# Four graph layers on one core: the adjacency products of the last two layers with features stationary and the adjacency moving

## The reference

```
1: relu((I - D A_sym D) (h W))                          A_sym = relu((A + A.T) / 2)
2: softmax over neighbours(leaky(s1 + s2)) (h W)
3: h = relu(A (h Wg0 + bg0)); h = relu(A (h Wg1 + bg1))
   then four LSTMs over windows of 1, 2, 3, 4 nodes write parts of h anew
4: A_hat = dinv (A + I) dinv; z = (A_hat h) W1.T
   out = batchnorm(relu(batchnorm(z)) W2.T)
```

## Time and profile before

| | us |
|---|---|
| median of 3 runs | 3378.92 (3371.41 to 3380.02) |
| the profiled execution | 3374.21 |
| its span in the profile | 3372.0 |

### The profile page before, as it was taken

One profiled execution on the slowest core, in us unless ns is written; L12 is line 12 of the kernel. 1 busy time (PEld: TensorE's weight loads), 2 busy tenths in 40 slices (PEclk: granted clock), 3 DMA queues, 4 the chain that ended last, 5 costly groups with the idle time before them and its releaser, 6 DMA issues. The chain is left out here.

```text
span 3372.0 us, 39977 instructions
## 1 busy us (share of the span) xinstructions
PE 2826.8 (84%) x14962; PEld 2369.5 (70%) x14962; DVE 1708.4 (51%) x2868; ACT 1273.6 (38%) x2136; POOL 222.4 (7%) x121
## 2 busy tenths in 40 slices
PE   1328999859899994999979999698989885999977
PEld 1216888759899993788867878576768674777743
DVE  3874454456767663222232222388787874333336
ACT  3763222245555553111121111266767664111115
POOL 0220111100000100000000000001000000000000
PEclk8558999979999996999989999899999997999979
DMA  7875333231322224111132111301121025223238
GB/s 293 291 264 201 131 122 139 89 132 39 109 67 63 76 56 157 70 57 63 68 144 82 56 63 67 119 13 38 26 75 50 26 63 189 93 94 118 100 129 315
DMA packets 237887, 366.34 MB, mean 109 GB/s; under 512 B 8752, under 2 KB 190272, under 8 KB 216896
## 3 DMA queue, kind: packets, MB, share of 16 engines
q1 hardware_dynamic: 235456, 360.51, 31.2%
q10 hardware_dynamic: 2304, 4.20, 0.3%
HBM read 226.12 MB, written 138.55 MB: 108 GB/s over the span
## 5 line engine op out<-in xcount | busy, mean ns | idle before, releaser
L1040 PE MATMUL n_acc<-n_hb,n_p 128*128 128x129 f32 x4096 | 484.5, 281 | 47.5 <-DVE n_u L998 30.9
L1040 PEld LDWEIGHTS n_acc<-n_hb,n_p 128*128 128x128 f32 x4096 | 478.4, 197 | 49.0 <-issue 28.5
L679 PE MATMUL l_acc<-l_g_hi,l_a_hi 128*128 128x512 f32 x1024 | 336.1, 410 | 86.7 <-DVE l_g_lo L587 80.7
L1620 ACT ACTIVATE r_gate<-r_ps,r_bias 128x512 f32<-128x512 f32 (+2 forms) x504 | 296.7, 638 | 108.4 <-PE r_ps L1761 76.8
L982 DVE SCALAR_TENSOR_TENSOR n_p<-n_e,n_cols,c_mT 128x2048 f32<-128x2048 f32 x128 | 296.0, 2346 | 81.9 <-ACT n_e L952 59.8
L679 PE MATMUL l_acc<-l_g_lo,l_a_hi 128*128 128x512 f32 x1024 | 318.7, 393 | 0.0
L679 PE MATMUL l_acc<-l_g_hi,l_a_lo 128*128 128x512 f32 x1024 | 317.6, 391 | 0.0
L679 PEld LDWEIGHTS l_acc<-l_g_hi,l_a_hi 128*128 128x128 f32 x1024 | 189.4, 190 | 140.4 <-issue 90.8
L952 ACT ACTIVATE n_e<-n_row,n_cols 128x2048 f32<-128x2048 f32 x128 | 260.1, 2083 | 26.8 <-DVE n_p L982 15.3
L534 ACT ACTIVATE l_a_hi<-l_a_raw 128x2048 fp32r<-128x2048 f32 x32 | 61.3, 1917 | 495.2 <-DMA l_a_raw<-adjT 327.1
L679 PEld LDWEIGHTS l_acc<-l_g_hi,l_a_lo 128*128 128x128 f32 x1024 | 193.8, 189 | 41.7
(11 more groups left out here) (239 smaller groups left out, 4831.3 us busy)
## 6 DMA issues: line engine op xcount, KB each, us to landing
l_ht<-h SPq DMA_DIRECT2D x48, 512.0 KB, 6.8
a_sb<-in_adj_dram SPq DMA_DIRECT2D x16, 1024.0 KB, 21.7
adjT<-at SPq DMA_DIRECT2D x16, 1024.0 KB, 4.3
anorm<-an SPq DMA_DIRECT2D x16, 1024.0 KB, 3.9
l_a_raw<-anorm SPq DMA_DIRECT2D x16, 1024.0 KB, 6.3
l2a_a_raw<-adjT SPq DMA_DIRECT2D x16, 1024.0 KB, 5.2
l2b_a_raw<-adjT SPq DMA_DIRECT2D x16, 1024.0 KB, 5.8
l_a_raw<-adjT SPq DMA_DIRECT2D x16, 1024.0 KB, 6.5
```

Of the source, the lines that this page charges most:

```text
L679: last = pe.matmul(acc[:, t.par, c * 512:(c + 1) * 512], lhs[:, t.par, s], rhs[:, s, c * 512:(c + 1) * 512], start=(s == 0 and lhs is a_hi ...
L1040: last = pe.matmul(acc[:, k, o:o + D + 1], pr[:, j % DEPTH, t * P:(t + 1) * P], hb[:, b.par, j], start=(j == 0 and o == 0), stop=(j == T - 1),
L1620: act.activation(gate[k][:, g, 0:size], ps[k][:, g, 0:size], ACT.Tanh if g == 2 else ACT.Sigmoid, bias=bias[:, 2, units[n].p - 1, g:g + 1] ...
```

## The change

A new function `spread` replaces `product` in layers 3 and 4; "l0" keeps `product`. The host hands over `adjT`, the transposed adjacency cut into 4 column chunks (CH) x 16 pieces of [128, 512], so `prepare` no longer stores a transpose. `spread` goes by chunks of 512 output nodes. For each chunk it takes the 16 pieces one after the other through a ring of four; for each piece 8 batches x 3 matmuls run, with the batch's feature tile stationary and the piece moving, and the sums of the 8 batches fill the 8 PSUM banks. The sums come out with features on the partitions: no transpose. After piece 15 the banks are copied to `ut` (ACT the even ones, DVE the odd ones; in layer 4 DVE all, times `row`), PE projects in place into the same banks, and results leave through a ring of 6 buffers `res` of [128, 512] to DRAM. The two products of layer 3 are two jobs of one call: the features of the second replace those of the first while its last chunk runs. In layer 4 the unit matrix is added on DVE to the pieces on the diagonal, and one row scaling by `dinv3` happens in `ut`. `perceptron` reads `z1` in the same shape with its columns in another order, and its last ACT loop is written out.

```diff
@@ prepare @@
-                        sp.wait_ge(copied, t.n * 2 + 2)
-                        sp.dma_start(io["adjT"][t.n], at[:, t.par]).then_inc(at_out[t.par], 16)
...
-                            act.wait_ge(at_out[u.par], u.pair * 16)
+                            act.wait_ge(masked, u.n - 1)
@@ new function @@
+CH = 4
+CW = N // CH
+RING = 4
+def spread(prog, io, keep, name, jobs):
...
+    UNITS = {"L2a": 8, "L2b": 8, "L3": 16}
+    OUT = 6
...
+        g_hi = prog.sb(ctx, n_("g_hi"), [P, T, W], F32R)
+        g_lo = prog.sb(ctx, n_("g_lo"), [P, T, W], F32R)
+        raw = prog.sb(ctx, n_("raw"), [P, RING, CW])
+        hraw = prog.sb(ctx, n_("hraw"), [P, 2, W])
+        res = prog.sb(ctx, n_("res"), [P, OUT, CW])
+        acc = prog.ps(ctx, n_("acc"), [P, B, CW])
...
+        def h_after(gp):
+            if gp < T:
+                return [gp]
+            return [h for h in range(T, J * T) if gp == ((h // T) * PIECES - T + h % T + RING if h % T < 12 else
+                                                         (h // T) * PIECES + RING + 2 + h % T - 12)]
+        def ended_at(gp):
+            return gp // T - 1 if gp % T == RING - 2 and gp >= T else None
...
@@ spread, sync @@
+            def piece(gp):
+                if gp >= RING:
+                    sp.wait_ge(a_low, gp - RING + 1)
+                sp.dma_start(raw[:, gp % RING], io["pieces"][gp % PIECES // T, gp % T]).then_inc(raw_in[gp % RING], 16)
+            def features(h):
+                if h >= 2:
+                    sp.wait_ge(g_low, h - 1)
+                if h >= T:
+                    for g in range(2):
+                        u = units_at[h // T * CH - CH + h % T // CH] + g * CH + h % CH
+                        sp.wait_ge(res_out[u % OUT], 16 * (u // OUT + 1))
+                sp.dma_start(hraw[:, h % 2], jobs[h // T]["h"][h % T].rearrange("p b f -> p (b f)"))\
+                  .then_inc(h_in[h % 2], 16)
...
+            for gp in range(TOTAL):
+                piece(gp)
+                if gp >= T and gp % T == RING + 2:
+                    store(gp // T - 1)
+                for h in h_after(gp):
+                    features(h)
+                if gp == 3:
+                    weights()
...
@@ spread, scalar @@
+            def finish(ch):
+                kind = kind_of(ch)
+                if kind == "L3":
+                    for r in range(16):
+                        u = units_at[ch] + r
+                        act.wait_ge(projected, u + 1)
+                        if u >= OUT:
+                            act.wait_ge(res_out[u % OUT], 16 * (u // OUT))
+                            act.wait_ge(po_read, u - OUT + 1)
+                        act.activation(res[:, u % OUT], acc[:, r % 8], ACT.Copy).then_inc(res_ready, 1)
+                    return
+                for b in range(0, B, 2):
+                    act.wait_ge(summed, ch * B + b + 1)
+                    act.activation(ut[:, b], acc[:, b], ACT.Copy).then_inc(copied[0], 1)
...
@@ spread, vector @@
+            def finish(ch):
...
+                for b in range(B) if kind == "L3" else range(1, B, 2):
+                    dve.wait_ge(summed, ch * B + b + 1)
+                    if kind == "L3":
+                        dve.tensor_tensor(ut[:, b], acc[:, b], cols, ALU.mult).then_inc(copied[0], 1)
+                    else:
+                        dve.tensor_copy(ut[:, b], acc[:, b]).then_inc(copied[1], 1)
...
+                    if u >= OUT:
+                        dve.wait_ge(res_out[u % OUT], 16 * (u // OUT))
...
@@ spread, tensor @@
+            def chunk(ch):
+                n, c = chunks[ch]
+                for s in range(T):
+                    gp = ch * T + s
+                    if c == 0:
+                        pe.wait_ge(g_low, n * T + s + 1)
+                    pe.wait_ge(a_low, gp + 1)
+                    for b in range(B):
+                        if s == 0 and ch:
+                            pe.wait_ge(res_ready if deep else po_read, units_at[ch] - B + b + 1)
...
+                        for lhs, rhs in ((g_hi, a_hi), (g_hi, a_lo), (g_lo, a_hi)):
+                            last = pe.matmul(acc[:, b], lhs[:, s, b * D:(b + 1) * D], rhs[:, gp % RING],
+                                             start=(s == 0 and lhs is g_hi and rhs is a_hi),
+                                             stop=(s == T - 1 and lhs is g_lo))
...
+            def project(ch):
...
+                    if kind == "L2a":
+                        g, j = r // CH, r % CH
+                        pe.wait_ge(copied[0], ch * 4 + g * 2 + 2)
+                        pe.wait_ge(copied[1], ch * 4 + g * 2 + 2)
+                        for b in range(4):
+                            last = pe.matmul(acc[:, r, b * D:(b + 1) * D], ut[:, g * 4 + b, j * P:(j + 1) * P],
+                                             wsb[n][:, :], start=True, stop=True)
+                    elif kind == "L2b":
+                        pe.wait_ge(copied[r % 2], ch * 4 + r // 2 + 1)
+                        last = pe.matmul(acc[:, r], wsb[n][:, :], ut[:, r], start=True, stop=True)
+                    else:
+                        k, b = r // 8, r % 8
+                        pe.wait_ge(copied[0], ch * 8 + b + 1)
+                        if k:
+                            pe.wait_ge(res_ready, units_at[ch] + b + 1)
+                        last = pe.matmul(acc[:, b], wsb[n][:, k * P:(k + 1) * P], ut[:, b], start=True, stop=True)
...
@@ network @@
-        product(prog, io, keep, "l2a", io["adjT"], io["h2"], dict(w=wg0, b=bg0), "L2a")
-        product(prog, io, keep, "l2b", io["adjT"], io["h2b"], dict(w=wg1, b=bg1), "L2b")
+        spread(prog, io, keep, "l2", [dict(kind="L2a", h=io["h2"], w=wg0, b=bg0),
+                                      dict(kind="L2b", h=io["h2b"], w=wg1, b=bg1)])
         recurrences(prog, io, keep, dict(wih=wih, whh=whh, bih=bih, bhh=bhh))
-        product(prog, io, keep, "l3", io["adjT"], io["h3"], dict(w=w1), "L3")
+        spread(prog, io, keep, "l3", [dict(kind="L3", h=io["h3"], w=w1)])
```

More of the change, by code:

```diff
@@ L260, in prepare @@
             an_out = prog.sems("an_out")
-            at_out = prog.sems("at_out")
             mask_out = prog.sems("mask_out")
@@ L287, in _ @@
                 sp.dma_start(io["rsrow"], keep["rsT"][0:T, :]).then_inc(rs_out, 16)
-                for s in at_out + an_out + mask_out + h_out:
+                for s in an_out + mask_out + h_out:
                     sp.wait_ge(s, 16 * HALF)
@@ L1870, in final @@
                     act.wait_ge(aff_own, 18)
-                act.activation(y[:, t.par], o2[:, t.n], ACT.Identity, bias=aff[:, 2, 1:2],
+                c, j = t.n // CH, t.n % CH
+                o = o2[:, c * CH:c * CH + CH, :].rearrange("p q (b n) -> p (q b) n", n=CW)[:, :, j * P:(j + 1) * P]
+                act.activation(y[:, t.par].rearrange("p (b n) -> p b n", n=P), o, ACT.Identity, bias=aff[:, 2, 1:2],
                                scale=aff[:, 2, 0:1]).then_inc(y_ready, 1)
-            run_slots(act, final, T, 2, 2)
+            for t in range(T):
+                final(Tile(t))
         @block.vector
@@ L1919, in _, with network @@
             run_slots(pe, final, T, 2, 2)
-def network(nc, x, adj, w0, wa, wcT, wc, wg0, bg0, wg1, bg1, wih, whh, bih, bhh, w1, w2, vec, out):
+def network(nc, x, adj, adjT, w0, wa, wcT, wc, wg0, bg0, wg1, bg1, wih, whh, bih, bhh, w1, w2, vec, out):
     with ExitStack() as ctx:
@@ L1927, in network @@
             io[name] = nc.dram_tensor(name, [T, P, B, D], F32).ap()
-        for name in ("adjT", "anorm"):
-            io[name] = nc.dram_tensor(name, [T, P, T, P], F32).ap()
+        io["anorm"] = nc.dram_tensor("anorm", [T, P, T, P], F32).ap()
+        io["pieces"] = adjT
+        io["d3row"] = nc.dram_tensor("d3row", [T, P], F32).ap()
         io["mT"] = nc.dram_tensor("mT", [T, P, T, P], U8).ap()
@@ L1963 @@
         "adj": a["adj"][node][:, node],
+        "adjT": a["adj"][node][:, node].T.reshape(T, P, CH, CW).transpose(2, 0, 1, 3),
         "w0": a["L0_gnn_W"],
```

180 lines of the change are left out of this document (added).

## The result

The changed kernel takes **3261.28 us** (median of 4 runs, 3259.83 to 3263.04) against 3376.57 of the kernel before on the same chip: ratio 0.9661, 95% interval 0.9645 to 0.9676, 115 us less. The prediction said 3290, with 3250 to 3318 as its range. The number that came in is that of rival (a), 3260: the adjacency stream kept its old pace. The range holds it because (a) had set the range's lower end.

The account below looks back on a forecast made before the run. PE's list of work, plus the places where PE stands still, was taken to bound the rewritten stages. From the profiled 3374.2 us, 54.0 for the third layer and 30.5 for the fourth came off: 3290, range 3250 to 3318.

Parts of the forecast that it names:

- rival (a): Adjacency products of layers 3 and 4: the old pace of 0.2267 us a matmul holds, 30 us less, 3260; chance 0.36.
- Transposes, 12.6 us a product: Three adjacency products: 16 x 0.79 us of transposes on PE's path go in each, 38 us in all.
- Waits at the start of a product, costed at nothing: Start of each product: feature supply stays ahead of PE, so no waits; without that cover the old 10 us return per product.
- The border between the products: Third layer: the second product's features enter during the first's last chunk, so the old border, PE starting at 1748.18 after 1736.7, goes.
- The pace of the main stream: 4608 matmuls of the adjacency products: three writes to one bank make them 0.2333 us each instead of 0.2267, 30 us.
- Projections and borders: Between chunks: projections of 6.8, 6.9 and 13.8 us, no bubble, 0.4 us allowed a border for restarting the stream.
- Entries: From stage start to first matmul: 7.0 us in the third layer (was 10.5), 10.0 in the fourth (was 10.4).
- ends: Behind the last matmul: 13.5 us in the third layer (was 11.4), 17.7 in the fourth (was 26.4).
- Rival (b), evacuation: Chunk borders: PE waits until DVE and ACT have emptied all banks, 118 us at ten borders, 3408; chance 0.03.
- Rival (d), a closer issue: Main stream: with nothing but streaming between matmuls the pace is 0.215 us, 84 us less, 3206; chance 0.02.
- Elsewhere, nothing: First stage's dropped store costed at nothing, ends -5 and +1; final affine step nothing, +-1; straight-line code nothing.
- (c): Small waits at ten borders (store ring, late features, slower first chunk), 2 to 3 us each, 3310 to 3320; chance 0.07 with (e).

Follow-up runs that it names:

- the repetition: The changed kernel as it is, run again beside two others on another chip than the first comparison: 3256.04 us, ratio 0.9642.
- the first stream test: All stages left out, only TensorE streams of 256 matmuls with other operands and bank orders: 226.7 ns a matmul, 233.4 with the shifted tile.

## Why the prediction was right, and where it was off

- **Transposes, 12.6 us a product:** right, shown by the run that tripled them.
- **Waits at the start of a product, costed at nothing:** right by the traces; no run takes this term by itself. The first chunk's 384 matmuls take 88.8 us (1321.05 to 1409.85) and a later one's 86.9; the 1.9 us between them are nine matmuls at the lower clock level, for which the sum had 1.6. In the repetition they were fourteen, 2.8 us.
- **The border between the products:** right; the run with two stages puts 9 to 12 us on it.
- **The pace of the main stream:** the step that failed. "I take 0.2333, the row whose order is the new one." The order had nothing to do with it. At 0.2267 the sum's 3072 and 1536 matmuls come to 696.4 and 348.2 us, 20.3 and 10.1 less, so the forecast would have been 769.2 and 420.1 against 767.4 and 419.1 measured. The prediction was 29 us too high, and this one term is 30. The rest cancels: in the profile the two layers came out 2.8 us under this corrected sum, the stages counted as unchanged 6.3 over. The run with 32 bytes of padding, 28.6 us slower than the changed kernel, is the forecast with another cause. Rival (a), at 0.36, had the right number and a clue that the order of banks might not be the cause: the slow pace also shows where banks alternate. That clue is another effect. Those ten matmuls stand behind fp32 passes, both tiles lie at equal addresses, and in the first stream test such a slow start behind fp32 passes also dies out, after six. No term of the sum had the address: that the old and the new product both have their tiles at 32 is the luck of the allocation.
- **Projections and borders:** 7.06 us a border measured against 6.8 + 0.4; in the second product 6.9 (6.47 from 1786.87 to 1793.34 and 0.40 by which the second matmul comes late, as it does behind the fp32 passes of the stream test, where nothing is waited for) against 6.9 + 0.4; in the fourth layer 13.7 against 14.2. The allowance for a restart was not needed. Entries 6.7 and 9.5 (7.0, 10.0), ends 13.3 and 18.0 (13.5, 17.7).
- **Rival (b), evacuation:** the changed kernel doesn't do it. Built in a run of its own, it made the kernel slower, as forecast, but by 184 and not 118: some 30 us are copies and results that it priced too cheaply or at too few places, the rest is the clock, lower behind the pauses of 5 us. The Trainium skill (Perfetto Trace Analysis, Optimization Strategy) says that such recurring gaps can mean a want of PSUM or SBUF; in the changed kernel there is no gap, and in the serial one the same eight banks are just as full. Here the grain of the waits decided, not the room.
- **Rival (d), a closer issue:** no pace of 0.215 showed up anywhere. The Trainium skill (TensorE: Matmul & The Clock Gate, Back-to-back issue gap) has 216 ns for 512 columns in its isolated formula; every stream here, with a weight load of its own for each matmul, ran at 226.7 or slower.
- **Elsewhere, nothing:** right for the store. The recurrences and the last stage, which differ by 1.8 and 4.5 us in the first pair of profiles, differ as much between profiles of kernels that are alike there.
- **Two slips without weight:** DVE and ACT do not work for "a quarter of it or less" in all three stages; in the fourth layer DVE is busy for 165 of 461 us, 36%. And the middle of (c) plus 4.7 is 3320, not 3318.

## What to carry to other kernels

When a stage elsewhere in the trace is the only row for a new pace, list everything in which it differs before one difference is named the cause; a stream test of half a dozen variants costs one run and would have settled 30 us here. Results in PSUM can be emptied without a spare bank, if each bank has its own wait and the engines take the banks in the order in which they finish. And in such a stream PE should not stand still for 5 us, because here such a pause was paid twice, the second time in the clock. Last, look at where the allocator puts the tiles that PE reads together: one small tile between them cost 28.6 us here.

## What the runs showed of the hardware

The pace of fp32r matmuls of 512 columns depends on where the moving and the stationary tile lie in a partition: 226.7 ns when their byte addresses agree modulo 256, 233.4 for differences (moving less stationary) of 32, 96, 128, 192 and 224, 234.2 for 160, 229.0 for 64; with the moving tile 4, 8, 16, 36, 48, 68 and 80 bytes off the seven streams' mean was 233.9. Only these differences were measured, each in streams of 128 matmuls of one execution, and multiples of 256 that separate the tiles made no difference. At equal addresses the pace does not depend on the values (dense, sparse, zeros), on the order of banks, or on what ACT and DVE do meanwhile: from the twentieth matmul of a chunk on, the changed stream's distances are 226.7 on average beside running splits, as in the stream test without them. The Trainium skill (SBUF — State Buffer, SBUF: two separate sides) says that PE never waits on another engine there, and this trace agrees, with that 226.7. Why the difference of the two addresses counts is open: no run here looked inside.

The lower level of the clock shows behind pauses of PE: after 5.54 us without work matmuls of 512 columns start 0.43 us apart instead of 0.227, after 5.16 and 5.01 us fp32 passes of 512 columns start 0.85 apart instead of 0.43. After 2.76 us the passes of 128 columns ran 0.11 apart, as at the full clock.
